# Sort stage of a graph network kernel: how edge keys come in, where the half projections stand, which operation builds the one-hots, and how the padding is written

## What is computed

```python
h = jnp.maximum(_layernorm(x, axis=-1), 0.0)
# message passing: for every edge
msg_input = jnp.concatenate([h[src], h[dst], edge_attr_16], axis=-1)
m = jax.nn.relu(msg_input @ mW1 + mb1) @ mW2 + mb2
agg = jax.ops.segment_sum(m, src, num_segments=3125)
x = x + h + relu(concat([h, agg]) @ uW1 + ub1) @ uW2 + ub2
h = jnp.maximum(_layernorm(x, axis=-1), 0.0)
# three graph convolutions with the normalised adjacency, gelu between them, and x added
```

## Time and profile before

| | before |
|---|---|
| median of 3 runs | 2592.73 us (2592.11 to 2595.55) |
| the profiled execution | 2615.53 us, its span 2613.7 us |
| busy: PE / DVE / ACT / POOL | 2058.4 / 1706.8 / 813.2 / 1208.2 us |
| granted TensorE clock, mean | 0.866 |
| first to last scatter of the sort stage (L353) | starts 77.8 to 672.2 us |
| the edge stage's first transfer | 702.45 us |

### The profile page before, as it was taken

How to read it: one execution, slowest core, us unless ns; L and a number is a source line. 1 busy time by engine, 2 the same in 40 slices (tenths; PEclk the granted TensorE clock), 3 DMA queues, 4 the chain that set the end, 5 groups by cost and what they waited for, 6 DMA issues and landing times. The chain is left out here.

```text
span 2613.7 us, 38365 instructions
## 1 busy us (share of the span) xinstructions
PE 2058.4 (79%) x9517; PEld 1290.0 (49%) x9518; DVE 1706.8 (65%) x5026; ACT 813.2 (31%) x2430; POOL 1208.2 (46%) x1452
## 2 busy tenths in 40 slices
PE   2144445554399888889888889899997899999999
PEld 1122223332144333334333334677675688888887
DVE  4756666666577777777777778777776444444454
ACT  0111111111044444444444444455553410200100
POOL 0567777777344444444444443799985300000000
PEclk8566666666599999999999999899997899999999
DMA  7111111111144444444444443411111243344253
GB/s 253 57 40 39 43 41 45 42 42 39 48 132 130 128 126 131 129 135 133 127 127 131 127 134 106 129 61 59 57 63 55 93 121 111 104 126 120 83 155 96
DMA packets 187166, 255.86 MB, mean 98 GB/s; under 512 B 32646, under 2 KB 150992, under 8 KB 186976
## 3 DMA queue, kind: packets, MB, share of 16 engines
q0 software_dynamic: 45968, 119.96, 16.1%
q1 hardware_dynamic: 111944, 107.25, 13.9%
q10 hardware_dynamic: 29128, 27.14, 3.1%
HBM read 199.87 MB, written 57.50 MB: 98 GB/s over the span
## 5 line engine op out<-in xcount | busy, mean ns | idle before, releaser
L850 POOL DMA_INDIRECT brow<-B_rows,rows x416 | 396.4, 953 | 496.8 <-DVE pre L946 488.4
L353 POOL DMA_INDIRECT src_list<-ring,ring_row x392 | 442.3, 1128 | 201.9 <-issue 118.5
L1624 PE MATMUL pO<-F,y 128*128 128x512 f32 (+1 forms) x2100 | 473.7, 381 | 12.3 <-DVE y L1515 11.7
L888 PE MATMUL pNode<-hid,oh 128*128 128x512 f32 x832 | 452.7, 627 | 1.7 <-ACT hid L909 1.7
L1624 PEld LDWEIGHTS pO<-F,y 128*128 128x128 f32 x2100 | 372.4, 189 | 84.0 <-DVE y L1515 13.6
L909 ACT ACTIVATE hid<-pre 128x512 f32<-128x512 f32 x416 | 262.0, 630 | 407.1 <-DVE pre L946 406.3
L881 PE MATMUL pEdge<-A,turned 128*128 x1248 | 360.8, 399 | 0.0
L932 DVE TENSOR_TENSOR S<-S,pNode 128x512 f32 x416 | 285.6, 686 | 113.3 <-PE pNode L888 70.0
L946 DVE TENSOR_TENSOR pre<-pEdge,brow 128x512 f32<-128x512 f32 x416 | 282.1, 678 | 104.9 <-PE pEdge L881 104.8
L1485 DVE CAST F<-raw 128x512 fp32r<-128x512 uint16 (+1 forms) x525 | 205.9, 396 | 186.8 <-PE pO L1624 181.8
L1064 POOL TENSOR_SCALAR src_oh<-iota,src_s 128x128 bf16<-128x128 bf16 x473 | 304.6, 659 | 28.0 <-PE pC L1233 26.6
(11 more groups left out here) (277 smaller groups left out, 2965.1 us busy)
## 6 DMA issues: line engine op xcount, KB each, us to landing
raw<-C_rows SPq DMA_DIRECT2D x90, 640.0 KB, 4.0
C_rows<-c_rows ACTq DMA_DIRECT2D x175, 114.5 KB, 1.7
src_list<-fill SPq DMA_DIRECT2D x38, 275.0 KB, 4.6
rows<-src_list SPq DMA_DIRECT2D x104, 100.0 KB
brow<-B_rows,rows POOLq DMA_INDIRECT x416
B_rows<-bst SPq DMA_DIRECT2D x25, 256.0 KB
src_list<-ring,ring_row POOLq DMA_INDIRECT x392
hT_rows<-hT SPq DMA_DIRECT2D x25, 128.0 KB, 1.7
```

Source lines behind the costliest of these rows:

```text
L353: nc.gpsimd.indirect_dma_start(dr.src_list[:, :, :].rearrange("p t w -> (p t) w"), bass.IndirectOffsetOnAxis(ap=ring_row[:, k % RING, t:t ...
L850: nc.gpsimd.indirect_dma_start(brow[:, t % BR, :], None, dr.B, bass.IndirectOffsetOnAxis(ap=rows_i[:, b, j, 1:2], axis=0)).then_inc(b_in[t ...
L888: mm(pN[j % 2][:, :], oh32[:, (j - 2) % 4, :], hid[:, j % 2, :], start=True, stop=True).then_inc(node_done, 1)
L1624: last = mm(pO[n % 2][half][:, 0:width(c)], y_part(win, part, half), F[:, (n * NW + win) % FS, 0:width(c)], start=(win == 0 and part == 0) ...
```

## The change

The sort stage is rearranged; the other stages keep their code, shifted by 107 lines.

- Keys are loaded in transfers of 112, 15 and 1 partitions. The features are no longer copied to a DRAM table: each pair of blocks is loaded from the input, in the same three pieces, into a buffer that POOL zeroed once.
- DVE does the keys before the constants. `ck` comes from a multiply and a shift (3 operations for 6). The 26 one-hots of the second key are gone: `targets_of` builds the few it needs (`onehot_dst`, 175 columns) per block.
- `U` is built by 7 `tensor_scalar` operations of 182 columns in place of one `tensor_tensor` of 1274.
- Padding: one transfer writes the 25 tiles behind the first 391; then, once the histogram gives each window's last tile, 25 transfers of one tile each (13 from SP, 12 from ACT) write to an address read from registers. POOL waits for them before its first scatter.
- PE's order in a block is `move_on(k)`, `count_targets(k-4)`, `before(k+1)`, and only then the projections: `B` of the last window and the transposes in even blocks, `A` in odd ones. The bias enters `A` as a product of one row (L889) instead of DVE's addition `vA`.
- ACT makes `h` one block ahead and copies `hT` before `middle_parts`.
- Layer norm statistics are spread over blocks 1 to 3, and the tables are built in blocks 5 to 28 instead of behind the loop.

```diff
@@ start @@
+            sp.dma_start(key[0][0:EVENP, :], io["src"][0:EVENP * COLS].rearrange("(p t) -> p t", t=COLS)
+                         ).then_inc(src_in, 16)
+            sp.dma_start(key[0][EVENP:FULLP, :], io["src"][EVENP * COLS:FULLP * COLS].rearrange("(p t) -> p t", t=COLS)
+                         ).then_inc(src_in, 16)
...
-            for n in range(LT // FR):
-                sp.dma_start(dr.src_list[:, n * FR:(n + 1) * FR, :], fill[:, :, :]).then_inc(filled, 16)
...
+            sp.dma_start(dr.src_list[:, FULL_TILES:NT, :], fill[:, :, :]).then_inc(filled, 16)
...
+            for w in range(0, NW, 2):
+                sp.dma_start(dr.src_list[:, bass.ds(last[w], 1), :], fill[:, 0:1, :]).then_inc(last_filled, 16)
...
-            pool.wait_ge(filled, 16 * (LT // FR))
+            pool.wait_ge(last_filled, 16 * NW)
...
-            for c in range(2, CHK):
-                link(v.scalar_tensor_tensor(out=ck[:, :], in0=key[1][:, :], scalar=float(CW * c), in1=ck[:, :],
-                                            op0=ALU.is_ge, op1=ALU.add))
+            link(v.tensor_scalar(ck_i32[:, :], key[1][:, :], float(CK_MUL), None, ALU.mult))
+            link(v.tensor_scalar(ck_i32[:, :], ck_i32[:, :], CK_SHIFT, None, ALU.arith_shift_right))
+            link(v.tensor_copy(ck[:, :], ck_i32[:, :]))
@@ bins_of @@
-                v.tensor_tensor(U[:, k % 2, :, :], bin16[:, k * CH:(k + 1) * CH].unsqueeze(2).to_broadcast([P, CH, BINS]),
-                                bin_iota[:, :].unsqueeze(1).to_broadcast([P, CH, BINS]), ALU.is_equal
-                                ).then_inc(u_ready, 1)
+                for j in range(CH):
+                    v.tensor_scalar(U[:, k % 2, j, :], bin_iota[:, :], bin_f[:, k * CH + j:k * CH + j + 1], None,
+                                    ALU.is_equal).then_inc(u_ready, 1)
@@ PE loop @@
-                if k >= 1:
-                    move_on(k - 1)
-                before(k)
...
+                if k + 1 < BLOCKS:
+                    move_on(k)
+                else:
+                    pe.wait_ge(ranked, CH * BLOCKS)
+                if k >= TLAG + 1:
+                    count_targets(k - TLAG - 1)
+                if k + 1 < BLOCKS:
+                    before(k + 1)
```

More of the change, by code:

```diff
@@ L35 @@
 CW = 458
+CK_MUL = 1145
+CK_SHIFT = 19
 BINS = WINS * CHK
@@ L39 @@
 NS = -(-(NT + NW * (CHK - 1)) // 8) * 8
-LT = NT + 2
+LT = NT + 2 + NW
+FULL_TILES = -(-E // P)
 BANKS = 4
@@ L387, in _ @@
             upper_parts(0)
+            act.wait_ge(last_ready, 1)
+            act.wait_ge(filled, 16)
+            _, last = nc.values_load_multi_w_load_instructions(
+                last_w[0:1, :], engines=[act.engine], min_val=0, max_val=LT - 1,
+                skip_runtime_bounds_check_because="a source block's last tile, or a spare one of its own")
+            for w in range(1, NW, 2):
+                act.dma_start(dr.src_list[:, bass.ds(last[w], 1), :], fill[:, 0:1, :]).then_inc(last_filled, 16)
             for k in range(BLOCKS):
@@ L624, in _ @@
                     v.tensor_tensor(a_part(w, 2), rA[:, :], a_part(w, 1), ALU.subtract).then_inc(a_lo, 1)
-            for k in range(BLOCKS - 2, BLOCKS):
+            for k in range(BLOCKS - TLAG, BLOCKS):
                 targets_of(k)
@@ L657, in _ @@
-            link(v.tensor_tensor(turn_ck[:, 0:LASTB], ck_row[:, 1:BUCKETS], ck_row[:, 0:LASTB], ALU.subtract))
-            for n in range(2):
-                size = min(P, LASTB - n * P)
-                for q, row in enumerate((end_f, turn_tile, turn_ck)):
-                    link(v.tensor_tensor(diag[0:size, 0:size], row[0:size, n * P:n * P + size],
-                                         keep.ident[0:size, 0:size], ALU.mult))
-                    link(v.tensor_reduce(col[0:size, n, q:q + 1], diag[0:size, 0:size], AX.X, ALU.add))
-                link(v.tensor_scalar(ended[0:size, n, :], step_f[0:size, :], col[0:size, n, 0:1], None, ALU.is_ge))
-                for q in range(2):
-                    link(v.tensor_scalar(spread[0:size, n, q, :], ones[0:size, :], col[0:size, n, q + 1:q + 2], None,
-                                         ALU.mult))
@@ L748, in _ @@
                 if odd == 1 and 0 <= s < NW:
-                    pe.wait_ge(ht_ready, s + 1)
-                    if s >= 1:
-                        pe.wait_ge(va_ready, s)
-                        pe.wait_ge(b_ready, s)
                     if s == 0:
                         pe.wait_ge(w_in, 48)
-                    for out, n0 in ((pA, 0), (pB, 2)):
-                        for n in range(2):
-                            last = mm(out[:, :], hT[:, s % 2, n * P:(n + 1) * P], w1[:, n0 + n, :], start=(n == 0),
-                                      stop=(n == 1))
@@ L759, in _ @@
-                    last.then_inc(ab_done, 1)
-                if k >= 2:
-                    count_targets(k - 2)
-            for k in range(BLOCKS - 2, BLOCKS):
-                count_targets(k)
-            pe.wait_ge(tables_ready, 1)
-            pe.wait_ge(ht_ready, NW)
-            mm(pT[:, 0:NT], ones[0:NW - 1, :], ended_w, start=True, stop=True)
-            mm(pH[:, 0:BINS], ones[0:HP, :], same[0:HP, :, :].rearrange("p w c -> p (w c)"), start=True, stop=True
-               ).then_inc(tables_done, 1)
@@ L789, in _ @@
-            last.then_inc(tables_done, 1)
+                    if s >= 1:
+                        pe.wait_ge(ra_ready, s)
+                    mm(pA[:, :], ones[0:1, :], b1[0:1, :], start=True, stop=False)
+                    pe.wait_ge(ht_ready, s + 1)
+                    for n in range(2):
+                        last = mm(pA[:, :], hT[:, s % 2, n * P:(n + 1) * P], w1[:, n, :], start=False, stop=(n == 1))
+                    last.then_inc(a_done, 1)
+                tables(k)
+            for k in range(BLOCKS - TLAG - 1, BLOCKS):
+                count_targets(k)
```

478 lines of the change are left out of this document (287 added, 191 removed).

## The result

The changed kernel takes 2492.61 us (2487.03 to 2494.72, four runs) against 2593.24 (2592.11 to 2595.55, four runs): ratio 0.9608, 95% interval 0.9590 to 0.9625. The profiled execution took 2493.28 us. All but 1 us of the difference between the two profiled executions (122.3 us) lies ahead of the edge stage's first transfer.

What follows compares the result with a forecast made beforehand. The sort loop was taken as bound by POOL's stretched scatters against DVE and PE hand to hand; start 37.8, loop 62.4 and end 26.3 sum to 126.5 us, taken from the median 2592.73: 2466.2, range 2440 to 2508.

Steps and rivals of the forecast that it cites:

- Start: Ahead of the sort loop: earlier keys, fewer key passes and smaller padding bring the first scatter to 40, 37.8 us earlier.
- padding gates the start: Rival, chance 0.12: slow register loads and triggers put the first scatter at 50 to 56, total about 2480.
- Loop: First scatter to end of the last: POOL alone sets the pace, 533 us for 595.4, 62.4 less.
- Stretches: Sort loop: scatters made longer by DVE operations they begin inside, 25 us left of 63.2, bounds 12 and 63.
- waits: Sort loop: POOL's waits in the loop, 34.6 us before, taken as 10 (0 to 35).
- random place: Sort loop: a scatter every 1.3 us meets `onehot_lo` at a random place, expected loss 0.35 us.
- `U`'s part: Sort loop: the 38 us by which `U` stretches scatters go once it is seven `tensor_scalar`.
- End: Behind the last scatter: tables move under the loop, leaving 3 us of 29.27, so 26.3 less.
- its landing and the change of stage: 3: Behind the last scatter: only its landing and the change of stage remain, 3 us (2 to 6).
- I subtract the same from the median: Whole kernel: the 126.5 us saved from the profiled execution, 22.8 above the median, also come off the median 2592.73.
- DVE and PE both fit under POOL's 8.9: Sort loop, per block: DVE 7.9 us and PE 5.8 against POOL's 8.9, so POOL sets the pace.
- DVE and PE still set the pace: Rival, chance 0.14: late semaphore, `U` at 0.38 each or `ht_ready` holding PE; loop 575 to 590, total 2508 to 2523.

Runs made afterwards that it cites:

- r10: Changed kernel with its keys loaded in one transfer of 127 rows again, on the third chip: 2609.18 us, ratio 0.9938.
- e1: Changed kernel with `U` built by one `tensor_tensor` again, all else as changed: 2534.29 us, ratio 0.9770.
- e7: Changed kernel with `onehot_lo` also built by seven `tensor_scalar`, on the second chip: 2572.08 us, ratio 0.9803.
- e0: The kernel before, unchanged, profiled once more: 2597.73 us.
- r11: Changed kernel with ACT's order set back (`h` in its own even block, `hT` copied behind `middle_parts`), on the third chip: 2593.49 us, ratio 0.9889.
- e2: The kernel before with only `U` changed to seven `tensor_scalar`: 2589.97 us, ratio 0.9983.
- r8: Changed kernel unaltered, run once more on the third chip: 2601.03 us, ratio 0.9899.

## Why the prediction was right, and where it was off

The forecast of 2466.2 was 26.4 us (1.1%) too low; the measured 2492.61 lies in the range of 2440 to 2508. By its own steps:

- **Start, 37.8 predicted, 38.5 measured.** Each point was met within 0.7 us. The rival *padding gates the start* came true only in that payload and padding arrive together; it costs 0.3 to 0.6 us. That the keys are worth 12 of it is shown by r10 (12.0 us at the first scatter). There the trace agrees with the rule of the Trainium skill cited in the prediction (DMA: Bandwidth & Descriptors), by which 127 rows use one DMA engine: they move at a flat 25 GB/s.
- **Loop, 62.4 predicted, 63.3 measured.** Stretches 33.8 (25 taken), waits 2 (10 taken). The two terms missed by 9 and 8 in opposite directions; that the sum came out this close is luck. A scatter begins inside `onehot_lo` in 49 of 56 blocks; the random place that I reckoned with gives 48 (1.08/1.27 of 56). But each loses 0.58 us (28.6/49) where a random place in the operation gives 0.42 (0.95 squared over 2 x 1.08): scatters tend to begin near its start. That is 8 of the 9 us; why the phases stand so isn't shown. `U`'s part, 38 predicted, is 36 under `U` itself by e1's trace and 42 in its time.
- **`U` hardly holds POOL, but not for the reason given.** The prediction took it from L479 that a `tensor_scalar` doesn't hold a scatter. That row couldn't tell: of the five scatters beside L479 four began with 0.09 us of a piece left, less than the 0.13 that cost nothing, and one 0.04 us behind the start of the first piece. In after such operations do hold a scatter, to their end; what a piece of `U` can cost is small because it is short. The rule from the page SBUF — State Buffer of the Trainium skill, by which a `tensor_scalar` in a two-port mode locks GpSimd out for its whole length, isn't refuted, and the rows at 47.12 and 289.15 agree with it, as the one at 298.18 does with what the page says of operations with two SBUF inputs. The 11 us reckoned from it were too much: 55 scatters that began inside `U` were 1.0 us longer in all, and with e7's edit 50 inside the pieces of `onehot_lo` 0.65.
- **End, 26.3 predicted, 19.5 measured.** The step "its landing and the change of stage: 3" is the mis-sized term of the profiled sum: 9.8, of which 8.07 are POOL's DRAIN. Its row was in the trace before, hidden under the tables, and the sum of the end had no place for it. It makes 6.8 of the miss.
- **"I subtract the same from the median"** is the step that cost most, some 22 us. It took the 22.8 us between the profiled execution and the plain runs as an offset that the change leaves alone. But 17.5 of them lay in the very loop that the change shortens: e0, an execution of the same kernel near its median, has a loop of 577.9 us. Against that one the gains are 39.5 + 45.9 + 19.5 = 104.9 us (first scatter 78.8; from the last scatter to the edge stage 29.3), and 100.6 were measured. The changed kernel's profiled execution lies 0.7 us from its median.

"DVE and PE both fit under POOL's 8.9" held on the chip of the timed comparison and not on the other two. There the rival *DVE and PE still set the pace* comes out, with a loop of 613 to 638 us. Of its three reasons "a semaphore is late" is the one that the traces show, for PE's marks and without a cause; r11 shows that ACT's `hT` isn't it, and `U`'s pieces take 0.26 us there as in after, not 0.38. That the forecast stands on the chip of the timed comparison owes something to that chip: on the third the changed kernel's 2601.03 lie outside the range.

How much each part of the change is worth isn't a sum. e2 gives 4 us for `U` alone and e1 42 for the same edit with the rest in place.

## What to carry to other kernels

Where two loops of nearly the same length run against each other, a part that shortens one alone gives nearly nothing, and an execution's excess over the median may sit in the loop that is about to go: set a forecast against an execution near the median, or split the excess by stage first. An operation that holds another engine costs it what is left of that one instruction, so cutting it into short pieces helps. Before "X doesn't hold Y" is read from a few rows, look how much of X was left each time. Before work is moved out from behind a stage's end, list what every engine's sequencer does at that end, since what was hidden under the work becomes the new end. A gain measured on one chip by taking slack out of a chain of hand-overs can be a quarter as large on another, so such a change is worth running on a second chip.

## What the hardware showed that was not expected

- POOL's DRAIN at the end of the sort stage took 8.07 us in both kernels, and the first transfer of the next stage came 9.8 us behind the last scatter's end in every run without tables behind the loop, on all three chips.
- The same kernel took 2492.61 us on one chip and 2601.03 on another, with the three later stages within 3 us. The 105 us are waits in the sort loop for marks of PE, of which the one shown came 14.7 us behind its matmul's recorded start. The kernel before differs by 29 us between the two. In the slower traces a part of the semaphore records is missing (23671 in r8, 33136 in after; 26512 in the first profile of before, 32482 in e0), so the releasers there are named "remote".
- An indirect scatter that began inside a DVE operation with two SBUF inputs, a cast or a `tensor_scalar` lost what that operation had left, less 0.13 us (1.59 us under `onehot_lo`, 1.10 under a cast of 0.36; 0.967 undisturbed). It lost nothing where one input lay in PSUM, nor where the operation had begun under 0.03 us before it (130 scatters of the kept traces with over 0.2 us left); some pieces of `U` with 0.24 left didn't hold theirs either.
